# An LSTM over 6250 rows in rounds of 125 lanes: other rounds, and rows put in PSUM by ScalarE in all one-pass rounds

## What is computed

```python
x = x + _L0_gnn_ref(_layernorm(x), edge_index, W1, b1, W2, b2)
def step(carry, x_t):
    h_prev, c_prev = carry
    combined = jnp.concatenate((x_t, h_prev), axis=1)
    f_t = sigmoid(combined @ W_f + b_f)
    i_t = sigmoid(combined @ W_i + b_i)
    c_tilde = tanh(combined @ W_c + b_c)
    c_t = f_t * c_prev + i_t * c_tilde
    o_t = sigmoid(combined @ W_o + b_o)
    h_t = o_t * tanh(c_t)
    return ((h_t, c_t), h_t)
x = x + hs          # 6250 steps, batch 1, h and c have 512 numbers
```

## Time and profile before

| | us |
|---|---|
| median of 3 runs | 3029.12 (3022.49 to 3034.47) |
| profiled execution, span from first to last instruction | 3303.4 |
| of it before the first round | 1711.1 |
| "rough", "close", "full", "delta" (50 steps each) | 295.6, 305.6, 599.5, 341.6 |
| measuring and correcting after them | 8.6, 8.8, 14.9, 17.7 |

### The profile page before, as it was taken

How to read it: one execution, slowest core, us unless ns; L and a number is a source line. 1 busy time by engine, 2 the same in 40 slices (tenths; PEclk the granted TensorE clock), 3 DMA queues, 4 the chain that set the end, 5 groups by cost and what they waited for, 6 DMA issues and landing times. The chain is left out here.

```text
span 3303.4 us, 57302 instructions
## 1 busy us (share of the span) xinstructions
PE 2872.7 (87%) x11844; PEld 2116.3 (64%) x11845; DVE 2206.3 (67%) x5730; ACT 1745.7 (53%) x4557; POOL 996.9 (30%) x1008
## 2 busy tenths in 40 slices
PE   6967887888887988887869999999999999978786
PEld 5846665666665766665656666666677777755554
DVE  6746776767766766665757886666666666666665
ACT  4644444444444444444437776777344444447775
POOL 1135555555555655555540000000000000003332
PEclk9979988999898999988989999999999999989998
DMA  8556767677776777667666665664466656669997
GB/s 221 159 169 197 204 200 205 200 210 207 209 209 205 212 211 203 205 200 211 191 177 184 183 179 150 171 174 136 138 196 193 194 192 194 194 182 269 260 272 185
DMA packets 234635, 648.45 MB, mean 196 GB/s; under 512 B 65914, under 2 KB 87674, under 8 KB 203334
## 3 DMA queue, kind: packets, MB, share of 16 engines
q1 hardware_dynamic: 161768, 410.64, 42.8%
q0 software_dynamic: 72816, 237.24, 25.1%
HBM read 493.56 MB, written 154.16 MB: 196 GB/s over the span
## 5 line engine op out<-in xcount | busy, mean ns | idle before, releaser
L1474 PE MATMUL acc<-W_high,state 128*125 128x512 f32 x3200 | 998.3, 417 | 43.3 <-ACT acc L1407 38.7
L1474 PEld LDWEIGHTS acc<-W_high,state 128*125 128x125 f32 x3200 | 595.2, 191 | 242.1 <-ACT state L1354 57.1
L785 POOL DMA_INDIRECT rows<-ln_table,slab x400 | 409.5, 1024 | 467.0 <-issue 230.0
L1316 POOL TENSOR_TENSOR out<-h,lx 125x512 f32<-125x512 f32 x50 | 64.2, 1283 | 1394.0 <-DVE h L1753 1394.0
L785 POOL DMA_INDIRECT Wh<-ln_table,slab x400 | 406.1, 1015 | 217.5 <-issue 152.4
L819 ACT ACTIVATE high<-rows 128x512 fp32r<-128x512 f32 x400 | 243.6, 628 | 332.7 <-DMA rows<-ln_table,slab 225.6
L867 PE MATMUL agg<-high,onehot 128*125 128x512 f32 x800 | 347.8, 435 | 52.9 <-DVE low_part L976 38.0
L819 ACT ACTIVATE high<-Wh 128x512 fp32r<-128x512 f32 x400 | 241.3, 629 | 225.2 <-DMA Wh<-ln_table,slab 117.5
L867 PE MATMUL agg<-low_part,onehot 128*125 128x512 f32 x800 | 327.7, 410 | 0.0
L1474 PE MATMUL acc<-W_low,state 128*125 128x512 f32 x800 | 316.3, 395 | 0.0
L1733 DVE TENSOR_TENSOR fc<-gate,c 125x256 f32<-125x256 f32 x400 | 168.7, 422 | 210.4 <-ACT gate L1373 206.5
(11 more groups left out here) (217 smaller groups left out, 5032.7 us busy)
## 6 DMA issues: line engine op xcount, KB each, us to landing
xg<-gate_rows SPq DMA_DIRECT2D x150, 896.0 KB
gate_rows<-gout SPq DMA_DIRECT2D x200, 224.0 KB
total_rows<-total SPq DMA_DIRECT2D x50, 896.0 KB
xg<-total_rows SPq DMA_DIRECT2D x50, 896.0 KB
xg<-gate_rows SPq DMA_DIRECT2D x150, 104.0 KB
lx<-x_rows POOLq DMA_DIRECT2D x50, 250.0 KB, 8.2
out_dram<-out POOLq DMA_DIRECT2D x50, 250.0 KB, 8.3
h_steps<-hT SPq DMA_DIRECT2D x49, 250.0 KB, 2.6
```

What stands on the lines that cost most here:

```text
L785: e.indirect_dma_start(out=rows[j % RING][:, :], out_offset=None, in_=table[:, :], in_offset=bass.IndirectOffsetOnAxis(ap=slabs[j // SLAB] ...
L1474: m = e.matmul(acc[n][0:L, :], stationary[:, k, :], weights[:, k, n // 2, n % 2].rearrange("p s c -> p (s c)"), start=begins, stop=(k == K ...
```

## The change

The four rounds become "rough", "kept", "change", "final":

- "rough" runs steps 12 to 49 only. Gates, cell, tanh, decay and h are 16-bit tiles there (views of `total` and `h`), and turns are of 16 bits.
- "kept" takes the place of "full", as second round: h is rounded to 16 bits, so two passes (`W_high`, `W_low`) do instead of three, with no `h_low`. ScalarE keeps each turned h in the SBUF tile `kept`; `h_steps` and its DMAs are gone. Sums are stored as before.
- "change" and "final" both work as "delta" did, on the difference to what "kept" kept, and read the sums back; "final" also makes the output.
- All three one-pass rounds share one order on TensorE (`one_pass`), ScalarE writes the rows of banks 0 to 2, and VectorE those of bank 3. Except in the first step, no rows go by TensorE. In "rough" VectorE and not ScalarE makes `state`.
- `kept` takes 50,000 bytes a partition; `Wh` and some tiles of the earlier parts lie in it as views. `LOOSE` is larger, and the cell's gap counts a quarter in that comparison. `fc` is gone, and GpSimd clears three more tiles at the start.

```diff
-ROUGH = 2
+SKIP = 12
 TOLERANCE = 2.0 ** -17
-LOOSE = 2.0 ** -7
+LOOSE = 2.0 ** -3
+CELL_SHARE = 0.25
 
 
 
-        Wh = sb(top, "Wh", [P, K, 2, 2, 2, HALF])
+        kept = sb(top, "kept", [P, STEPS, K * LANES], F16)
+        Wh = (kept[:, :, :].rearrange("p t u -> p (t u)")[:, 0:2 * K * G4].bitcast(F32)
+              .rearrange("p (k a b s c) -> p k a b s c", k=K, a=2, b=2, s=2))
...
         total = [sb(ctx, f"total{n}", [P, 2, 2, PAIR]) for n in range(2)]
-        hT = [sb(ctx, f"hT{n}", [P, K, L]) for n in range(2)]
...
-        fc = sb(ctx, "fc", [P, K, P])
...
+        halves = [t[:, :, :, :].rearrange("p a b g -> p (a b g)").bitcast(F16) for t in total]
+        r_gate = halves[0][:, 0:G4].rearrange("p (a b s u) -> p a b s u", a=2, b=2, s=2)
+        r_c, r_ic, r_tc = (halves[1][:, n * D:(n + 1) * D].rearrange("p (k u) -> p k u", k=K) for n in range(3))
+        r_decay = halves[1][:, 3 * D:4 * D].rearrange("p (a u) -> p a u", a=2)
+        h_half = [t[:, :, :].bitcast(F16)[:, :, 0:P] for t in h]
...
+        def steps_of_round(e, kind, step):
+
+            begin = SKIP if kind == "rough" else 0
+            step(begin, 0, True, False)
+                    step(i * ROWS + (begin + n + 1), (n + 1) % ROWS, False, False)
...
-            for r, kind in enumerate(("rough", "close")):
-                steps(r, kind, 0)
-                measure(r, kind, 0)
-                correct(r, kind)
-            steps(FULL, "full", 0)
-            measure(FULL, "full", 0)
-            correct(FULL, "full")
-            steps(DELTA, "delta", 1)
-            measure(DELTA, "delta", 1)
+            for r, kind in enumerate(("rough", "kept", "change", "final")):
+                steps(r, kind)
+                measure(r, kind, {"kept": 0, "final": 1}.get(kind))
+                if kind != "final":
+                    correct(r, kind)
...
-                            e.activation(state[:, k, :], hturn[k][:, :], ACT.Copy).then_inc(s_state[k], 1)
-
-                    def keep(ks, s, par, summed):
+                            of = hturned_half[k] if kind == "kept" else hturned[k]
+                            e.activation(state[:, k, :], of, ACT.Copy).then_inc(s_state[k], 1)
+                    def keep(ks, s):
                         for k in ks:
-                            e.activation(hT[par][:, k, :], hturn[k][:, :], ACT.Copy).then_inc(s_kept[k // KH], 1)
+                            e.activation(kept[:, bass.ds(s + 1, 1), k * L:(k + 1) * L]
+                                         .rearrange("p o l -> p (o l)"),
+                                         hturned_half[k], ACT.Copy).then_inc(s_kept[k], 1)
...
+                    if kind == "kept":
+                        if not first:
+                            keep(SECOND, s - 1)
+                        new_cell(FIRST)
                         forget_input(1)
-                        new_cell(FIRST)
+                        if not last:
+                            take_turned(FIRST, now)
                         cell_gate(1)
                         output_gate(1)
+                        if not last:
+                            keep(FIRST, s)
+                        new_cell(SECOND)
...
-                    elif kind == "delta":
+                    else:
                         seed(0)
                         seed(1)
                         output_gate(1)
+                        new_cell(SECOND)
                         seed(2)
-                        seed(3)
-                    elif last:
-                        take_turned(SECOND, now)
...
-                    def delta_step():
-                        turn(FIRST, 1 - par, now - 1)
+                            turn(FIRST, 1 - par, now - 1)
                         seeded(1)
-                        product(1, 0)
-                        product(0, 0)
-                        product(0, 1)
-                        turn(SECOND, 1 - par, now - 1)
-                        for n, k in ((1, 1), (0, 2), (0, 3), (1, 2), (1, 3)):
+                        for n, k in ((0, 0), (1, 0), (0, 1), (1, 1)):
                             product(n, k)
                         seeded(2)
+                        for k in FIRST:
                             product(2, k)
+                        if not first:
+                            turn(SECOND, 1 - par, now - 1)
+                        for n in range(2):
+                            for k in SECOND:
+                                product(n, k)
                         seeded(3)
+                        for k in FIRST:
+                            m = product(3, k)
+                        if not first:
+                            m.then_inc(s_taken, 1)
+                        for n in range(2, 4):
+                            for k in SECOND:
+                                product(n, k)
+                    def two_passes():
...
+                        for n in range(3):
+                            e.wait_ge(s_sum[n], now - 1)
+                            products(n, FIRST, OF_HIGH, True)
+                        if not first:
+                            turn(SECOND, 1 - par, now - 1)
+                        for k in SECOND:
+                            stated(k)
                         for n in range(2):
-                            e.wait_ge(s_sum[n], summed - 1)
+                            products(n, SECOND, OF_HIGH, False).then_inc(s_acc[n], 1)
+                        e.wait_ge(s_sum[3], now - 1)
+                        products(3, FIRST, OF_HIGH, True)
+                        products(2, SECOND, OF_HIGH, False).then_inc(s_acc[2], 1)
+                        products(3, SECOND, OF_HIGH, False).then_inc(s_acc[3], 1)
+                        turn(FIRST, par, now)
+                        if last:
...
+                    def take_turned(ks):
+                            e.tensor_copy(state[:, k, :], hturned_half[k]).then_inc(s_state[k], 1)
+
+                    def moved(ks):
+                        for k in ks:
+                            e.wait_ge(s_turn[k], now)
+                            e.tensor_tensor(state[:, k, :], hturned[k],
+                                            kept[:, bass.ds(s + 1, 1), k * L:(k + 1) * L]
+                                            .rearrange("p o l -> p (o l)"),
...
+                        e.tensor_tensor(half_of(cell, half), gates[0:L, half, 0, 0].rearrange("c (k u) -> c k u", k=KH),
+                                        half_of(cell, half), ALU.mult).then_inc(s_prod[half], 1)
...
                         forgotten(1)
                         new_h(FIRST)
                         taken_in(1)
-                        if kind == "delta" and not last:
-                            moved(FIRST[:1], s, par, now)
+                        if not last:
+                            if kind == "rough":
+                                take_turned(FIRST)
                             new_cell(k)
-                        if kind == "delta" and not last:
-                            moved(FIRST[1:], s, par, now)
+                        if not last:
+                            if kind == "rough":
+                                take_turned(SECOND)
+                            else:
+                                moved(SECOND)
+                        if kind == "rough":
                             decayed()
-                        if kind == "rough" and not last:
+                        if not last:
                             seed()
```

More of the change, by code:

```diff
@@ L1294, in _, with steps @@
                                 ALU.subtract).then_inc(s_clear, 1)
-            def steps(r, kind, f):
-                if kind not in ("delta", "more"):
+            def steps(r, kind):
+                if kind not in ("final", "more"):
                     return
@@ L1343, in _, with steps @@
                 e.activation(W_high[:, k], Wh[:, k], ACT.Copy).then_inc(s_init, 1)
-            def steps(r, kind, f):
+            e.wait_ge(s_clear, CLEARED)
+            def steps(r, kind):
+                gates = r_gate if kind == "rough" else gate
+                cell, cell_turned = (r_c, r_tc) if kind == "rough" else (c, tc)
                 def step(s, q, first, last):
@@ L1438, in step @@
                         output_gate(1)
[L1439 to L1448 removed]
+                        new_cell(SECOND)
                         seed(2)
[L1450 to L1453 removed]
+                steps_of_round(e, kind, step)
+                if kind == "kept":
+                    for s in s_state:
+                        e.sem_inc(s, 1)
             def correct(r, kind):
@@ L1688, in after_own, with steps @@
                 ins.then_inc(s_own, 1)
-                e.wait_ge(s_own, own[0])
-            def steps(r, kind, f):
+                e.wait_ge(s_own, base[0] + own[0])
+            def steps(r, kind):
+                if kind == "rough":
+                    gates, cell, took, cell_turned, faded = r_gate, r_c, r_ic, r_tc, r_decay
+                else:
```

(19 more changed lines are left out.)

483 lines of the change are left out of this document (222 added, 261 removed).

## The result

2981.4 us (median of 4 runs, 2975.1 to 2987.2) against 3028.3 (4 runs): ratio 0.9846, 95% interval 0.9823 to 0.9868, so 47 us or 1.5% faster. Forecast were 2969 us in a range of 2905 to 3025, and faster.

What follows compares the result with a forecast made beforehand. TensorE was taken to bound rough, close and full, a loop through all engines delta. Kept -118, change +44, final +14, rough -3 and start +3 summed to -60 us, carried unscaled to 2969 us, range 2905 to 3025.

Steps and rivals of the forecast that it cites:

- kept, -118: Round full becomes kept: 16 of 48 products go, loop through VectorE sets a 9.47 us step instead of 11.87; round 481.9.
- the forecast's 2.46: In kept, time from bank 1's total to h: 2.20 us plus what bank 2's sum exceeds the tanh wait.
- rival D: Kept is held by its DMAs at full's rate, 10.6 us a step, +56: 3025, no difference; chance 0.09.
- change, +44: Round close becomes change: two products ahead of the turns enter the loop, step 6.88 us; round 349.8 against 305.6.
- the forecast's X+1.64: In a change step, bank 2's two products end 1.64 us after first product X, ahead of the second turns.
- final, +14: Round delta becomes final: the same 6.88 us step as change, plus 6 us of stalls kept; round 356.
- rough, -3: Rough: 12 steps of 5.65 us go, the others lengthen to 7.39 with a 32-bit decay of 0.69; round 292.2.
- Start, +3: Ahead of the first round: three more GpSimd memsets, +3 us, bounds 0 and 5.
- rival B: Gap over the bound on these inputs, so three-pass rounds of 600 us and more follow: about 3580; chance 0.04.
- Rival A: TensorE's clock gives way in one-pass rounds; 1.2 us on all 138 steps would cost 161: 3130; chance 0.09.
- 27 us that the forecast called stalls by DMA: In the old delta round, 322.0 us to step 48 against 294.7 undisturbed, put down to ScalarE awaiting input rows.
- Rival C: Faster: bank 2's row not felt (-35), kept near 8.4 (-52), 16-bit work quick (-10): about 2870 to 2900; chance 0.10.

Runs made afterwards that it cites:

- two runs that take away one or both: Changed kernel with ScalarE's bank 2 row ahead of the output gate: change steps 6.75 us; with bank 2's first two products behind the second turns: 6.28, ratio 0.958.
- the other pair of profiles: Profiles of the kernel before, unedited, in the first group (1584.9 us from the first round on) and the changed kernel again in the second (1535.5).
- delta order: Changed kernel with old delta_step's TensorE order in all one-pass rounds (three products ahead of second turns, bank 2 behind bank 1): ratio 0.946.
- fillers: Unread products closing one-pass steps: four on the changed kernel, 2956.4 us; two on delta order, rows by TensorE in rough and both kept edits, ratio 0.9348.
- the run with the row earlier: Changed kernel with ScalarE's rows of bank 2 ahead of the output gate, not at step end: steps 6.75 us in change and final, 6.80 in rough.
- the second group: Kernels run together on one chip; the changed kernel, unedited, measured 2978.3 us there against 3021.9 for the kernel before, ratio 0.9845.

## Why the prediction was right

By its steps, each in the rounds of the profiles:

- **kept, -118; measured -121.** The walk through VectorE gave 9.47, the trace 9.49, and each of its pieces came within 0.1. One was lucky as it stands: the sum of bank 2 was said to take 0.6 in a wait of 0.24, which leaves 0.36 and not the 0.26 in the forecast's 2.46; so written the step would be 9.57 and the round 5 us longer. The trace has 2.47, since VectorE starts an instruction up to 0.09 before the one ahead ends (the sum of 0.69 at 1905.27, h at 1905.87). That the sum ahead of h costs 0.25 was confirmed by moving it (9.23), and DMA, at 209 GB/s over the round, held nothing: rival D is out.
- **change, +44; measured +54.** The mechanism was right in both its pieces: the wait for bank 2's row (0.25) and the two products (0.47), by two runs that take away one or both. The step was 0.12 longer than 6.88: the turns came 0.11 later than the forecast's X+1.64, since the first product behind a wait keeps the next one waiting 0.33 and not 0.23 (its weight load starts only with the row, 2404.33), and the state took 0.06 more; 0.05 came back later in the step. That is 6 us. The other 5 are the four slow steps, which the sum had at nothing.
- **final, +14; measured +21.** The same two terms, less the 6 us of stalls that were kept in and hardly came.
- **rough, -3; measured -6.** Two errors that cancel, so that the near hit is luck. The median step was 7.07 and not 7.39, 12 us less in the round: decay in 16 bits is 0.42, not 0.69, and with that the sum would have had 7.12. Against it stand eleven slow steps: a mean of 7.37 without the first step, (7.37 - 7.07) x 36 = 11 us. The first step, 14.2 us, is not part of this; it took 15.5 before and stood in the 295.6 that the sum starts from; that it is 1.3 shorter is most of the rest. The Trainium skill (VectorE: DVE Perf Modes, "Mode 2×_1P — pack two bf16 into one 32-bit read") had 16-bit two-source operations at two a cycle; 0.42 us for 512 columns agrees with the estimate made from it. The forecast took the 32-bit row of the same operation as the nearest.
- **Start, +3; measured +2.4** (TensorE idles 14.65 us ahead of the first round's rows before and 17.09 after; in the other pair of profiles 15.25 and 16.43). Measuring and correcting took 1.5 us less.
- **Four rounds** were enough, so rival B is out.
- **Rival A came in part.** 19 slow steps of 138, at 1.3 us apiece in "change" and about 1 us in "rough", nowhere near the 51 from which the change would have been slower. What the forecast set against it was wrong, though: that the stretch without products, 1.95 us, was below the two of 2.12 and 2.15 in its rows. In the changed kernel that stretch is 1.91 us in each step and the clock falls in every twelfth or thirteenth step of "change", every eleventh of "final" and every third or fourth of "rough"; with 1.48 (delta order) it still fell 0 to 3 times a round; with fillers (1.2 and 1.14) never, and in the run with the row earlier, at 1.92, not once in "change" or "final". So the fillers end the falls, but the length of the stretch does not sort the runs, and neither does TensorE's busy share over "change" (0.76 with four slow steps, 0.79 with five, 0.75 with none). What does sort them stays open. The Trainium skill's rule (TensorE: Matmul & The Clock Gate, "A second HAM failure mode: psum-queue depth-cycling"), that idling between groups of matmuls makes the clock alternate, agrees with the slow steps seen here. The forecast also overlooked that the clock had cost something before: "delta" had a mean of 0.94, its trace has ten stretches at half the clock, and at the 1.17 us between the two steps of the earlier trace rows that is an estimate of 12 of the 27 us that the forecast called stalls by DMA.
- **Rival C** asked for bounds below the rows; kept's 8.4 wasn't near, the 16-bit gain came, the wait was felt.
- A slip on which nothing rests: a product's 0.23 us is for 512 columns and not the 500 of the forecast.

In all the forecast was -60, of which -63 from the first round on and +3 ahead of it. Measured were -53 from the first round on in these two profiles, 10 us less of a gain, and -47 in the medians (-49 and -44 in the second group). That 264 of the 274 us between profile and median lie ahead of the first round speaks for carrying the difference over unscaled; the forecast had no row for it.

## What to carry to other kernels

When a round of work is a loop through several engines, an instruction ahead of the hand-over (here two products and a wait for another engine's row ahead of the turns) costs its full length each step, while the same instruction behind the hand-over costs next to nothing as long as the engine would idle there: walk the loop once for each order. Where an engine idles in the loop, give it the work that another engine has on its path, as the rows in "rough". And when work is moved later on one engine, look at which in-order queue waits for its result, and what stands behind that wait.

## What the runs showed of the hardware

- What lies ahead of the recurrence took 1434 to 1447 us in some profiles and 1711 to 1772 in others, at 255 and 202 GB/s in the gather, for the same or nearly the same code; the recurrence of one and the same kernel agreed within 1% between them. A span with a profile is compared with runs beside it only.
- VectorE on 16-bit tiles with f16 in and out: 512 columns in 0.42 us against 0.69, 256 in 0.29 against 0.42, 128 in 0.22 against 0.29. The cast of 16-bit numbers from PSUM into `state` takes 0.28, as long as the 32-bit subtraction into it.
- In the first step of "rough" VectorE's products of 256 columns take 2.58 and 4.58 us, where they take 0.29 later. They end 0.15 us after the last two of GpSimd's four instructions for `W_low`, which end at 1455.41 and 1459.92. The kernel before has the same picture. No run moves `W_low` away, so that this is the cause is argued and not shown:

```profile
1446.19 13.73 POOL L1289 TENSOR_TENSOR W_low<-kept,W_high 128x2048 fp32r<-128x2048 f32 x3
1455.48 4.58 DVE L1751 TENSOR_TENSOR total<-total 125x256 f16<-125x256 f16 x1
```

- Four extra products a step that nobody reads made the kernel 22 us faster (2956.4 against 2978.3), through the granted clock: no step of the one-pass rounds has a fall with them, beside the first, and 18 have one without.
